# Value sums in thirds of a slab, and a ring of six PSUM banks for the attention-gram stage

## The reference, cut to what matters

```python
kv = jnp.einsum('oc,bchw->bohw', qkv_w, x)
kv = _dw3x3(kv, qkv_conv_w)
k, v = jnp.split(kv, 2, axis=1)
q = _ssl(x, conv5_w, conv7_w, conv9_w)
...
attn = jax.nn.softmax(jnp.einsum('bhdn,bhen->bhde', q, k) * temperature, axis=-1)
out = jnp.einsum('bhde,bhen->bhdn', attn, v).reshape(b, c, h, w)
```

## Time and profile before

| | us |
|---|---|
| median of 3 runs | 1373.13 (1371.81 to 1376.18) |
| profiled execution, its own time | 1372.45 |
| its span, first to last instruction | 1370.8 |
| TensorE busy | 1157.9 |
| VectorE busy | 1008.8 |
| ScalarE busy | 803.8 |

### The profile page before, as it was taken

How to read it: one execution, slowest core, us unless ns; L and a number is a source line. 1 busy time by engine, 2 the same in 40 slices (tenths; PEclk the granted TensorE clock), 3 DMA queues, 4 the chain that set the end, 5 groups by cost and what they waited for, 6 DMA issues and landing times. The chain is left out here.

```text
span 1370.8 us, 36304 instructions
## 1 busy us (share of the span) xinstructions
PE 1157.9 (84%) x12648; PEld 920.4 (67%) x12648; DVE 1008.8 (74%) x1801; ACT 803.8 (59%) x1414; POOL 533.8 (39%) x369
## 2 busy tenths in 40 slices
PE   0899937999999899998999999846999997999900
PEld 0555527889999899998999999724555554555500
DVE  6777517999999899998999999525777774163494
ACT  0677735777777676775777677202444445766382
POOL 6200004577687676876668686602000001000010
PEclk9999977999999999998999999866999999999955
DMA  9976783545544535445355354155777633000079
GB/s 325 416 298 262 296 196 88 138 108 123 148 106 120 136 93 147 132 99 137 98 135 144 102 132 112 40 211 185 248 262 262 231 92 121 1 0 0 1 300 406
DMA packets 148805, 221.21 MB, mean 161 GB/s; under 512 B 115746, under 2 KB 116892, under 8 KB 144296
## 3 DMA queue, kind: packets, MB, share of 16 engines
q1 hardware_dynamic: 137560, 152.23, 37.0%
q0 software_dynamic: 6480, 47.19, 9.1%
q10 hardware_dynamic: 4608, 19.67, 4.1%
HBM read 131.82 MB, written 87.20 MB: 160 GB/s over the span
## 5 line engine op out<-in xcount | busy, mean ns | idle before, releaser
L1693 PE MATMUL b_conv_bank<-b_sign,wsign 128*128 (+1 forms) x1728 | 299.7, 327 | 7.7 <-ACT b_sign L1491 7.5
L982 DVE SCALAR_TENSOR_TENSOR b_value_sum<-b_vin,b_vtaps,b_value_sum 128x576 f32<-128x576 f32 x320 | 259.3, 810 | 14.4 <-ACT b_value_sum L908 13.6
L1693 PEld LDWEIGHTS b_conv_bank<-b_sign,wsign 128*128 128x128 bf16 x1728 | 168.0, 97 | 144.6 <-issue 31.4
L936 ACT CAST b_feat<-b_bank 96x400 f16<-96x400 f32 x255 | 125.5, 492 | 184.9 <-PE b_bank L1026 184.9
L1024 PE MATMUL b_bank<-b_tkh,b_kt 96*96 96x100 f16 x1536 | 224.3, 211 | 2.5 <-DVE b_tml L1005 2.2
L1025 PE MATMUL b_bank<-b_tkl,b_kt 96*96 96x100 f16 x1536 | 223.7, 211 | 0.0
L1026 PE MATMUL b_bank<-b_tkh,b_kt 96*96 96x100 f16 x1536 | 223.7, 211 | 0.0
L1024 PE MATMUL b_bank<-b_yh,b_tmh 96*96 96x200 f16 x768 | 195.2, 254 | 30.8 <-DVE b_feat L989 11.0
L1024 PEld LDWEIGHTS b_bank<-b_tkh,b_kt 96*96 96x96 f16 x1536 | 195.2, 127 | 4.2 <-DVE b_tml L1005 2.5
L1026 PEld LDWEIGHTS b_bank<-b_tkh,b_kt 96*96 96x96 f16 x1536 | 195.3, 127 | 0.0
L1025 PEld LDWEIGHTS b_bank<-b_tkl,b_kt 96*96 96x96 f16 x1536 | 193.8, 126 | 0.0
(11 more groups left out here) (232 smaller groups left out, 2522.7 us busy)
## 6 DMA issues: line engine op xcount, KB each, us to landing
b_vin<-value_projection_scratch SPq DMA_DIRECT2D x32, 686.0 KB, 5.1
keys_scratch<-b_khl SPq DMA_DIRECT2D x24, 784.0 KB, 3.5
value_projection_scratch<-b_vout ACTq DMA_DIRECT2D x24, 784.0 KB, 4.7
b_kt<-keys_scratch SPq DMA_DIRECT2D x128, 147.0 KB, 3.3
b_xraw<-in_x SPq DMA_DIRECT2D x128, 144.0 KB, 4.8
values_scratch<-b_vacc SPq DMA_DIRECT2D x32, 576.0 KB, 3.2
values<-values_scratch SPq DMA_DIRECT2D x48, 384.0 KB, 3.7
out<-xs SPq DMA_DIRECT2D x25, 576.0 KB, 6.8
```

The lines of the kernel that those rows point to most:

```text
L936: nc.scalar.copy(*target(n, 0, k)).then_inc(s_hi, 1)
L982: nc.vector.scalar_tensor_tensor(whole if t == DVE_TAPS[-1] else part, src, vtaps[:, t:t + 1], part, ALU.mult, ALU.add).then_inc(s_tap, 1)
L1693: ins = nc.tensor.matmul(cbank[k % NBK][:, 0:CH].rearrange("p (r c) -> p r c", c=W), p["wsign"][nth // NIMG][:, t * C:(t + 1) * C], padded ...
```

## The change

The sums of the value convolution are made per third of a slab (4 rows, 384 columns) instead of per half. Such a sum fits one PSUM bank where the half needed two, and the bank that is left goes to the ring: NB is 6. There are 18 taps on VectorE and 3 seeds on ScalarE per slab instead of 12 and 2, at new places between the jobs. GpSimd's part is unchanged but for the counts it waits for.

```diff
-        NB = 5
-        HALF = SLAB // 2
+        NB = 6
+        PARTS = 3
+        PART = SLAB // PARTS
...
-        vsum = ctx.enter_context(nc.psum_tensor("b2_value_sum", [C, 2, 512], F32))
+        vsum = ctx.enter_context(nc.psum_tensor("b2_value_sum", [C, 512], F32))
...
-        NTAP = 2 * len(DVE_TAPS)
+        NTAP = PARTS * len(DVE_TAPS)
...
-        TAP_AT = (0, 2, 3, 5, 7, 8, 10, 12, 13, 15, 17, 18)
-        SEED_AT = (1, 11)
+        TAP_AT = (0, 1, 2, 3, 4, 4, 6, 7, 8, 9, 10, 11, 13, 14, 15, 16, 17, 18)
+        SEED_AT = (1, 7, 14)
...
-                pool.wait_ge(s_seed, i * 2 + 1)
+                pool.wait_ge(s_seed, i * PARTS + 1)
...
-                if half or not isinstance(i, int) or i:
-                    act.wait_ge(s_tap, i * NTAP + half * len(DVE_TAPS))
-                src = vin[:, slot, :].rearrange("p (r c) -> p r c", c=WP)[:, half * HALF:(half + 1) * HALF, 0:W]
-                nc.scalar.activation(vsum[:, :, 0:HALF // 2 * W].rearrange("p b (r c) -> p b r c", c=W),
-                                     src.rearrange("p (b r) c -> p b r c", b=2),
+                if part or not isinstance(i, int) or i:
+                    act.wait_ge(s_tap, i * NTAP + part * len(DVE_TAPS))
+                nc.scalar.activation(vsum[:, 0:PART * W].rearrange("p (r c) -> p r c", c=W),
+                                     vin[:, slot, :].rearrange("p (r c) -> p r c", c=WP)[:, part * PART:(part + 1) * PART, 0:W],
                                      ACT.Copy, scale=vtaps[:, 0:1]).then_inc(s_seed, 1)
...
-                nc.vector.scalar_tensor_tensor(whole if t == DVE_TAPS[-1] else part, src, vtaps[:, t:t + 1], part,
+                nc.vector.scalar_tensor_tensor(done if t == DVE_TAPS[-1] else total, src, vtaps[:, t:t + 1], total,
                                                ALU.mult, ALU.add).then_inc(s_tap, 1)
...
-                    if n in TAP_AT:
+                    for _ in range(TAP_AT.count(n)):
                         tap(k, i, m, pairs + (k // 2 + 1))
                         m += 1
```

More of the change, by code:

```diff
@@ L898, in high_x, with seed @@
                 nc.scalar.copy(xh[0][:, slot, :, :, :].rearrange("h b c w -> h (b c w)"), xraw[:, slot, :]).then_inc(s_xh, 1)
-            def seed(k, i, half, loads):
+            def seed(k, i, part, loads):
                 slot = k % 2
-                if half == 0:
+                if part == 0:
                     act.wait_ge(s_vin[slot], loads * 16)
-                if half or not isinstance(i, int) or i:
-                    act.wait_ge(s_tap, i * NTAP + half * len(DVE_TAPS))
-                src = vin[:, slot, :].rearrange("p (r c) -> p r c", c=WP)[:, half * HALF:(half + 1) * HALF, 0:W]
-                nc.scalar.activation(vsum[:, :, 0:HALF // 2 * W].rearrange("p b (r c) -> p b r c", c=W),
-                                     src.rearrange("p (b r) c -> p b r c", b=2),
+                if part or not isinstance(i, int) or i:
+                    act.wait_ge(s_tap, i * NTAP + part * len(DVE_TAPS))
+                nc.scalar.activation(vsum[:, 0:PART * W].rearrange("p (r c) -> p r c", c=W),
+                                     vin[:, slot, :].rearrange("p (r c) -> p r c", c=WP)[:, part * PART:(part + 1) * PART, 0:W],
                                      ACT.Copy, scale=vtaps[:, 0:1]).then_inc(s_seed, 1)
@@ L968, in tap @@
             def tap(k, i, m, loads):
-                slot, half, t = k % 2, m // len(DVE_TAPS), DVE_TAPS[m % len(DVE_TAPS)]
-                src = vin[:, slot, :].rearrange("p (r c) -> p r c", c=WP)[:, half * HALF + t // 3:(half + 1) * HALF + t // 3,
+                slot, part, t = k % 2, m // len(DVE_TAPS), DVE_TAPS[m % len(DVE_TAPS)]
+                src = vin[:, slot, :].rearrange("p (r c) -> p r c", c=WP)[:, part * PART + t // 3:(part + 1) * PART + t // 3,
                                                                           t % 3:t % 3 + W]
-                src = src.rearrange("p (b r) c -> p b r c", b=2)
-                whole = vacc[:, slot, half * HALF * W:(half + 1) * HALF * W].rearrange("p (b r c) -> p b r c", b=2, c=W)
-                part = vsum[:, :, 0:HALF // 2 * W].rearrange("p b (r c) -> p b r c", c=W)
+                done = vacc[:, slot, part * PART * W:(part + 1) * PART * W].rearrange("p (r c) -> p r c", c=W)
+                total = vsum[:, 0:PART * W].rearrange("p (r c) -> p r c", c=W)
                 if t == DVE_TAPS[0]:
-                    dve.wait_ge(s_seed, i * 2 + (half + 1))
+                    dve.wait_ge(s_seed, i * PARTS + (part + 1))
                 else:
```

## The result

The changed kernel takes 1475.91 us (median of four runs, 1471.44 to 1477.09), the kernel before 1374.16 in the same count; the ratio is 1.0735, with a 95% interval of 1.0706 to 1.0764. The profiled execution took 1477.09 us, with a span of 1475.5. One of the twelve executions of experiment 6 took 1477.58 us at a mean granted clock of 0.81, where its others had 0.93 to 0.94: its ratio leaves that one out, its median takes it in.

What follows compares the result with a forecast made beforehand. The prediction saw TensorE and VectorE both close to full in the grams stage, with VectorE to be the bound. 1372.45 + 63.3 (full-clock slabs) + 58 (clock falls) = 1493.8, stated as 1494 us; eight-in-ten range 1430 to 1522.

Steps and rivals of the forecast that it cites:

- The boundary wait: At each slab's start TensorE's job 0 waits for the previous slab's split 18, starting about 0.06 us after its end.
- The tap at 0.52 us and a second stretch of 14.7: On VectorE, 384-column taps 0.52 us apart; start of split 4 to end of split 18 grows from 13.53 to 14.7 us.
- The first stretch of 7.7 us as a fixed chain: From job 0's start on TensorE to VectorE's split 4, through ScalarE's copies and normalising: 7.7 us at full clock.
- The sum at full clock: Slabs of 0.06 + 7.7 + 14.7 = 22.46 us whatever their grams; 63.3 us added over the stage, 45 to 100.
- The gaps: TensorE's idle time before job 0: 3.7 us without gram matmuls there, 2.7 with, some 1.3 in some slow-starting slabs.
- About 20 new falls of the clock: Among the 28 slabs starting at full clock before, about 20 would newly start slow; bounds 0 and 28.
- 2.9 us for each: Price of a clock fall in a slab's first stretch, 10.56 against 7.7 us; 20 falls make 58 us, bounds 0 to 81.
- forecast was 1.1, for slab 31: In the stage's last slab, 1.1 us added, as part of the 63.3 us at full clock.
- The stretched rule: The skill page's half-clock start of each burst, applied to TensorE at every slab: all 28 fall, 1517 us, chance 0.12.
- The rival of 1411 us: Slab boundaries cost only TensorE's lost lead, mean 1.35 us in 28 slabs, the taps' extra hidden; chance 0.08.
- That of a clock that holds (1436 to 1451): Rival: TensorE's clock mostly holds through the boundary gaps, 63 us added and at most five falls; chance 0.27.
- The gain that a sixth bank could bring: Rival: job 0's wait isn't felt and TensorE's 19.2 us of waits for splits vanish, 1354 us; chance 0.03.

Runs made afterwards that it cites:

- experiment 6: Changed kernel with its six banks in an evenly spread table and ScalarE's normalising moved from job 4 to job 10: 1379.46 us, ratio 1.0033 to the kernel before.
- Experiment 3: Kernel before, halves and five banks, with TensorE made to wait before each slab's job 0 for the previous slab's split 18: 1433.26 us, ratio 1.0423.
- experiment 1: Changed kernel with its six banks taken from a table where none returns before the fifth job, across the slab's end too: 1381.32 us, ratio 1.0032.
- experiment 4: Changed kernel with 16 or 30 matmuls whose result nobody reads in TensorE's gap before job 0: 1442.93 us, ratio 1.0481 to the kernel before.
- Experiment 5: Kernel before with ScalarE's normalising of the next slab moved from job 4 to job 10: 1370.71 us, ratio 0.9977.
- experiment 2: Changed kernel with the old ring of five banks, keeping thirds, 18 taps and 3 seeds: 1381.66 us, ratio 1.0045 to the kernel before.

## Why the prediction was right, and which term was mis-sized

The range held the time, and the mechanism was the one forecast. The forecast of 1494 was 18 us too high, and one term, the price of a fall of the clock, was 17.8 us too high; the smaller errors of the others (2.5 too high, 3.7 too low) nearly cancel.

- **The boundary wait** (job 0 not before the end of split 18): right, 0.05 to 0.06 us behind it, 30 times of 31. Experiment 3 shows it as a cause by itself (58 us with its own gaps), experiment 1 that without it nearly nothing is left.
- **The tap at 0.52 us and a second stretch of 14.7:** right, 609 ns, 0.52 and 14.63 to 14.76.
- **The first stretch of 7.7 us as a fixed chain:** right at full clock (7.7 to 7.9, in the changed kernel and in experiment 4). Experiment 5 shows that normalising sets its last 0.65 us; what lies under it is 7.0 us.
- **The sum at full clock:** 62.2 us had been forecast for slabs 0 to 30. Their job-0 starts, first to last, lie 747.0 us apart where it was 647.1 before, 99.9 more; 40.2 of that is first stretches above 7.7 in newly slow slabs (below), which leaves 59.7. The two loop turns cost nothing (22.55 us where 22.55 and 22.71 were), not 0.6 each.
- **The gaps:** forecast 3.7, 2.7, and some 1.3 after four gram pieces; measured 3.61, mostly 2.2 to 2.4, and 1.24 to 1.41.
- **About 20 new falls of the clock:** 20. That some boundaries would have a gap of only 1.3 us and keep the clock was argued and came true (1.24 to 1.41 us, seven slabs); that the count is exact is luck, since of the two gaps between, 1.60 us (slab 21) came with a fall and 2.03 us (slab 25) didn't. By the trace, slabs 2 to 6, 8 to 10, 13, 14, 16 to 18, 21, 22, 24, 26, 28 to 30.
- **2.9 us for each: this step failed.** I took the price from slabs 12, 1 and 20, the only slow ones there were. It held in six of the 20 slabs (10.3 to 11.1 us of first stretch); in 14 the stretch was 9.1 to 9.35 us, 1.4 to 1.65 above 7.7. Together 40.2 us, or 2.0 each, against 58. In these 14 the clock fell only 0.1 to 1.7 us after job 0 had begun, and it was low for under 4 us. So it was in slab 9 (job 0 at 431.36), where it was back 5 us after job 0:

```profile
431.50:432.50 1.00, 1.00 (x13) 1.00 (x13) 0.74 (x2) 0.00 (x0) 0.34 (x1) 1.00 0.00 0
433.00:436.00 3.00, 3.00 (x39) 3.00 (x37) 1.11 (x2) 0.97 (x2) 2.82 (x2) 0.50 0.00 0
436.50:440.00 3.50, 3.50 (x66) 3.39 (x65) 3.22 (x6) 3.50 (x8) 3.21 (x2) 1.00 0.02 5
```

The low stretch lies between 432.5 and 436.5, where the earlier trace rows show 0.50 for all of 6 us in slab 12 before. In the loops of the kernel before the three low stretches were all longer (6.8 to 10 us), behind gaps of 3.65 us and more. But its trace did hold one as short, at gram matmuls behind the stage's last slab, which the prediction didn't use:

```profile
886.00:889.00 3.00, 0.05 (x1) 0.00 (x0) 0.00 (x0) 0.71 (x1) 2.82 (x5) 1.00 0.16 36
889.60:892.80 3.20, 3.20 (x17) 2.28 (x16) 0.00 (x0) 0.00 (x0) 0.54 (x1) 0.50 0.00 0
893.00:899.00 6.00, 4.63 (x66) 3.92 (x64) 0.00 (x0) 1.15 (x2) 0.00 (x0) 1.00 0.01 3
```

- **Outside these slabs** the span grew by 104.7 - 99.9 = 4.8 us; forecast was 1.1, for slab 31. The stage starts 1.3 us later; the other 3.5 lie in slab 31 and behind.

The rule of the Trainium skill (page "TensorE: Matmul & The Clock Gate", section "HAM oscillation — how this bites in real kernels") was stretched by the prediction to every burst behind any wait. The kernel described there waits some 3 to 5 us for a DMA before each burst, and the gaps here were mostly shorter. The stretched rule was too strong: in 23 of slabs 1 to 30 the clock was low at job 0 or fell within 1.7 us of it, and after gaps up to 1.41 us it held. On the other side it fell here with every gap of 2.2 us or more, shorter than the waits of that section. Experiment 4 shows that the fall is a cost in its own right and not a mark of the wait: with the same wait and a loop of 22.4 us the clock stays at 1.00, and the time is 33 us less.

The rival of 1411 us (lost lead only, the tap's extra hidden) has its first half in experiment 3: at full clock the wait costs 37.5 us, about the lost lead (37.8). Its second half fails. The changed kernel's cost at full clock is 59.7 us, so behind the wait thirds cost some 22 us, where without it they cost 6 (experiment 2), and no fall of the clock was in that rival at all. That of a clock that holds (1436 to 1451) is what experiment 4 makes. That its 1442.93 us lies in that range is partly chance: the late matmuls at three boundaries add 15 us, and slabs 1, 12 and 20 give 9.6 back. The gain that a sixth bank could bring, 19.2 us of waits, does not come even when the ring is even (experiment 1): by then VectorE is as full as TensorE, and these waits are 27.0 us.

## What to carry to other kernels

A ring of n buffers in a loop body of J jobs, with the buffer chosen by the job's number in the body, is only as long as its shortest distance: write down the distance to the last use for each job, across the body's end too. Here six banks gave a distance of two at one point, and that point decided. And where an engine that runs ahead is made to wait for one that it used to lead, price the closed loop (from the release to the work that leads to the next release), then look at what the new gap does to TensorE's clock; here the fallen clock made 40 of the 102 us lost. An instruction that is moved into an engine's idle time wants its length compared with that idle time: normalising took 2.4 us, and the place it was moved to had idled 1.7 to 1.95.

## What the runs showed of the hardware

The clock did not need a gap as long as the 3.65 us of the kernel before. At the changed kernel's boundaries the clock fell in or within 1.7 us behind every gap of 2.2 us or more (22 slabs), and behind none of 1.2 to 1.4 us (seven); it fell at one of 1.60 and not at one of 2.03. In experiment 3 it fell at two of seven gaps of 1.59 us. The same gap can go either way.

Matmuls that served nothing (16 or 30 of 200 columns in each gap) gave 33 us back in all. Where the gap had been short and the clock had held, they changed nothing (slab 7 took 22.56 us with and without them); at the three boundaries where they came late, at half clock, they cost some 5 us each.
